# Four PSUM banks for the score products, and a new order of the first and last row blocks, in a two-layer graph kernel

## The chip, the cores and the metric

One core of one Trainium2 chip. The metric is the device time of one execution in microseconds; the median of three runs before the change is 658.79 us (658.75 to 659.19).

## The reference

`x` is 4096 x 128, `adj` is 4096 x 4096 with zeros and ones, `N` is 4096.

```
deg  = clip(adj.sum(1), 1);  dis = deg ** -0.5
diffusion = (dis[:, None] * adj * dis[None, :]) @ x - x
sim  = x @ x.T / (norms[:, None] * norms[None, :])
attn = softmax(beta * sim * adj, axis=1)
L0   = diffusion + sigmoid(alpha) * (attn @ x - x)
x    = layernorm(x + L0)
L1   = relu(adj @ (x @ weights))
out  = layernorm(x + L1)
```

## The kernel before, in words

Rows are handled in 32 **row blocks** `r` of 128 rows. Everything that belongs to an even block has `q = 0`, to an odd one `q = 1` (buffers of two). One row block of the attention goes through these steps; the name is that of the helper in the code, with its line.

- `land_piece` (SyncE, L242) brings a quarter of the block's adjacency rows into `land`. `cast` (ScalarE, L482) turns each quarter into bytes in `adj_bytes` and counts `cast_done`.
- `sign_block` (GpSimd, L321) makes the stationary operand. `cosines(r, q, h)` (TensorE, L1005) computes 512 columns of the scores of block `r` with three matmuls into one PSUM bank, for `h` from 0 to 7.
- `mask(r, q, h)` (VectorE, L708) multiplies that bank by the adjacency bytes into `scores` and counts `scores_done`. It waits for the cosines (`s_done`) and for the cast of its quarter, number `r*4 + h//2 + 1`. After eight of them `row_max` (L717, L719) gives the maximum.
- `exps` (ScalarE, L523) takes the exponential, a quarter at a time in the order 2, 3, 0, 1 (0, 2, 3, 1 in the first and last block).
- Half of the exponentials, `b` from 0 to 3, is transposed by TensorE: `turn_e` (L1016) into `ps_e[0]` or `ps_e[1]`, then split into a high and a low fp16 part by `e_high` (ScalarE, L530) and `e_low` (VectorE, L723). The other half is split first, by `ex_high` (GpSimd, L351) and `ex_low` (VectorE, L729, both tensor inputs in SBUF), and transposed by a DMA, `turn_ex` (SyncE, L254), into `eTx`.
- `attend(r, q, k)` (TensorE, L1038 and L1041) multiplies piece `order[k]` of the block by `x_parts`. `attn_add` (VectorE) adds the sum to `u`.
- `pack` (GpSimd, L331 to L343) and `turn_adj` (SyncE, L248) keep a packed, transposed adjacency matrix for the later phases.

From block 2 on these steps stand in a loop of two row blocks per turn, on every engine; in `row` TensorE issues, for each `h`, a `turn_e` (even `h`), one `cosines` of a block ahead and one `attend` of a block behind. The first blocks and the last two are written out by hand. Work that exists once stands among the first ones: `x_split`, `x_high` (GpSimd, L355 to L364) and `x_low(1)` (VectorE, L760, both tensor inputs in SBUF) make `x_parts`; `first_attend(2)` waits for `x_low(1)`. `minus_x` (GpSimd, L370) writes the start value of `u` in four pieces, and VectorE waits for all four before it enters its loop:

```
            row(1, 1, second=True)
            dve.wait_ge(u_init, C)
            with dve.Fori(2, R - 15, 2) as r:
```

After the attention come the diffusion sums (`sums` and `whole_row` on TensorE), the first normalisation, and the second layer (`z_rows`, `z_w`). `first_sums(i)`, the first of these, needs `y_low(i)` (VectorE, L819), which needs `y_high` (ScalarE) and `y_rows` (GpSimd, L443, both inputs in SBUF). They are issued among the last two row blocks, beside `late_attend` (block 30) and `last_attend` (block 31).

PSUM has eight banks: `ps_s[0..1]`, `ps_e[0..3]`, `ps_acc`, `ps_at`. In the first block scores go to `ps_s` and to `ps_e[0..3]`; from block 1 on to `ps_s[h % 2]` alone, so that `cosines` number `n` waits for `mask` number `n - 2`. `ps_e[2]` and `ps_at` are then unused until the sums.

## Time and profile before

| | us |
|---|---|
| median of 3 runs | 658.79 |
| the profiled execution, its own time | 658.59 |
| its span, first to last instruction | 656.7 |
| TensorE busy | 638.0 (97%) |
| VectorE busy | 517.8 (79%) |
| ScalarE busy | 412.2 (63%) |
| GpSimd busy | 236.8 (36%) |
| granted TensorE clock | 0.998 |

All times below are microseconds from the start of the span. The attention fills the first 427 us, of which the hand-written start is about 55 and the hand-written end about 25. Masks, `e_low` and `exps` in the rows below are told apart by their order in the code. A matmul's end is modelled; a step from one start to the next is the better measure of what TensorE takes.

### The profile page before, as it was taken

How to read it: one execution, taken by the hardware profiler on the slowest of the kernel's cores; microseconds unless marked ns; L12 is line 12 of the kernel's file. 1: busy time of each engine (PE TensorE's matmuls, PEld its weight loads, DVE VectorE, ACT ScalarE, POOL GpSimd, SP SyncE). 2: the span in 40 equal slices, each digit the busy share in tenths (PEclk: the TensorE clock that was granted, in tenths of full speed). 3: DMA queues.
4: the chain of work that ended last, by engine and by line, in shares of the span. 5: the costliest groups of instructions: out<-in, count | busy, mean ns of one | idle time of the engine just before them, and what ended most of it. 6: DMA issues, size and time to landing. Idle time of an engine off the chain costs nothing.

```text
span 656.7 us, 16155 instructions
## 1 busy us (share of the span) xinstructions
PE 638.0 (97%) x5087; PEld 463.5 (71%) x5087; DVE 517.8 (79%) x1565; ACT 412.2 (63%) x768; POOL 236.8 (36%) x249
## 2 busy tenths in 40 slices
PE   7788999999999999999999999999999999999996
PEld 6456777777777777777777777888888864444465
DVE  4987999999999999999999998878777773334443
ACT  6998999999999999999999998612111110000000
POOL 5998553553554554544544546400000000000000
PEclk9999999999999999999999999999999999999999
DMA  7878999999999999999999996300000000000000
GB/s 282 303 161 215 278 272 239 279 256 253 280 267 239 285 263 233 285 263 242 292 258 240 307 237 97 77 1 1 0 0 0 0 0 1 16 17 16 16 33 33
DMA packets 165019, 107.36 MB, mean 163 GB/s; under 512 B 144384, under 2 KB 148608, under 8 KB 164992
## 3 DMA queue, kind: packets, MB, share of 16 engines
q1 hardware_dynamic: 164992, 107.04, 61.6%
q8 instruction: 12, 0.20, 0.1%
q14 instruction: 15, 0.12, 0.1%
HBM read 69.27 MB, written 2.10 MB: 109 GB/s over the span
## 4 chain that ended last, share of the span: by engine, by line
PE 86%; DVE 4%; DMA 4%; ACT 2%; issue 2%; POOL 1%; DVEq 0%; SPq 0%; POOLq 0%; ACTq 0%
PE ps_s L1005 22%; PE ps_s L1198 17%; PE ps_e L1170 15%; PE ps_e L1016 8%; PE ps_e L1038 8%; PE ps_acc L1038 7%; PE ps_e L1041 4%; PE ps_acc L1041 4%; DMA eTx<-e_parts 2%; DVE scores L708 1%; DMA x_keep<-in_x 1%; PE ps_e L1054 1%; DVE e_parts L729 1%; PE ps_acc L1182 1%; PE ps_s L1054 1%
## 5 line engine op out<-in xcount | busy, mean ns | idle before, releaser
L1005 PE MATMUL ps_s<-xn_parts,xn_signed 128*128 128x512 f16 x756 | 203.3, 379 | 4.2 <-DVE cmax L708 4.2
L708 DVE CUSTOM_DVE_ANT_1 scores<-ps_s,adj_bytes 128x512 f32<-128x512 f32 x252 | 171.6, 683 | 24.4 <-PE ps_s L1005 15.2
L523 ACT ACTIVATE scores<-scores,col 128x1024 f32<-128x1024 f32 x128 | 157.4, 1232 | 2.1 <-DVE col L719 1.9
L482 ACT ACTIVATE adj_bytes<-land 128x1024 uint8<-128x1024 f32 x128 | 133.5, 1047 | 0.6 <-POOL packed L343 0.6
L351 POOL TENSOR_SCALAR e_parts<-scores 128x1024 f16<-128x1024 f32 x64 | 68.5, 1071 | 157.7 <-ACT scores L523 154.2
L1170 PE MATMUL ps_e<-y_parts,stage 128*128 128x256 f16 x896 | 98.0, 273 | 0.0
L1005 PEld LDWEIGHTS ps_s<-xn_parts,xn_signed 128*128 128x128 f16 x756 | 68.4, 98 | 40.2 <-DVE cmax L708 4.3
L1170 PEld LDWEIGHTS ps_e<-y_parts,stage 128*128 128x128 fp8e4 x896 | 87.7, 98 | 10.1
L530 ACT ACTIVATE eT_parts<-ps_e 128x512 f16<-128x512 f32 x128 | 75.8, 595 | 28.7 <-PE ps_e L1016 27.9
L723 DVE SCALAR_TENSOR_TENSOR eT_parts<-ps_e,eT_parts 128x512 f16<-128x512 f32 x128 | 87.4, 683 | 1.9 <-ACT eT_parts L530 1.9
L729 DVE SCALAR_TENSOR_TENSOR e_parts<-scores,e_parts 128x1024 f16<-128x1024 f32 x64 | 88.4, 1382 | 0.4 <-POOL e_parts L351 0.4
L1016 PE MATMUL ps_e<-ident,scores 128*128 128x128 f32 x512 | 77.0, 274 | 1.6 <-ACT scores L523 1.6
L619 ACT ACTIVATE scores<-ps_s 128x512 f32<-128x512 f32 (+1 forms) x9 | 4.9, 550 | 108.6 <-PE ps_s L1198 108.6
L596 ACT ACTIVATE std<-mv,col 128x1 f32<-128x1 f32 x32 | 9.4, 295 | 84.2 <-DVE mv L898 84.2
L1016 PEld LDWEIGHTS ps_e<-ident,scores 128*128 128x128 f32 x512 | 53.9, 140 | 4.4 <-ACT scores L523 1.6
L1198 PE MATMUL ps_s<-stage,x_parts 128*128 128x512 fp8e4 (+1 forms) x320 | 56.9, 336 | 0.0
L1198 PE MATMUL ps_s<-land,x_parts 128*128 128x512 fp8e4 x256 | 56.4, 379 | 0.0
L805 DVE TENSOR_SCALAR stage<-packT 128x256 uint32<-128x256 uint32 (+1 forms) x192 | 42.6, 287 | 14.7 <-PE ps_e L1170 11.8
L1038 PE MATMUL ps_acc<-x_parts,eT_parts 128*128 128x256 f16 x256 | 49.0, 273 | 1.6 <-DVE eT_parts L723 1.6
L340 POOL TENSOR_TENSOR packed<-packed,adj_bytes 128x256 uint32<-128x256 uint32 x48 | 49.1, 1023 | 2.7
L1038 PE MATMUL ps_e<-x_parts,eT_parts 128*128 128x256 f16 x256 | 49.0, 273 | 0.6 <-DVE eT_parts L723 0.6
L1038 PE MATMUL ps_acc<-x_parts,eTx 128*128 128x256 f16 x256 | 48.9, 273 | 0.6 <-DMA eTx<-e_parts 0.6
(128 smaller groups left out, 967.1 us busy)
## 6 DMA issues: line engine op xcount, KB each, us to landing
land<-in_adj SPq DMA_DIRECT2D x128, 512.0 KB, 5.4
x_keep<-in_x SPq DMA_DIRECT2D x4, 512.0 KB, 5.6
out<-u SPq DMA_DIRECT2D x7, 256.0 KB, 2.1
eTx<-e_parts SPq DMA_TRANSPOSE x64, 4.3
packT<-packed SPq DMA_TRANSPOSE x16, 6.5
out<-u SPq DMA_DIRECT2D x2, 128.0 KB, 1.7
scores<-in_L_gnn_weights SPq DMA_DIRECT2D x1, 64.0 KB, 2.0
col<-in_L_gnn_beta SPq DMA_DIRECT2D x1, 0.5 KB, 7.1
```

The costliest lines, as they stand in the source:

```text
L351: nc.gpsimd.tensor_scalar(e_parts[:, n, 0, :], scores[:, q, (n + 2) * CH:(n + 3) * CH], E_SCALE, 1.0, ALU.mult, ALU.mult).wait_op(sign_don ...
L482: nc.scalar.activation(adj_bytes[:, q, i * CH:(i + 1) * CH], land[:, q, i, :], ACT.Copy, scale=float(BYTE_TOP[q] >> i), accum_out=deg[:, i ...
L523: nc.scalar.activation(piece, piece, ACT.Exp, bias=neg_max[q], scale=abs_beta, accum_out=csum[:, q, i:i + 1]).then_inc(exp_done, 1)
L530: nc.scalar.activation(eT_parts[:, b, 0, :], ps_e[:, b % 2, :], ACT.Copy, scale=E_SCALE).then_inc(e_hi, 1)
L708: nc.vector.tensor_tensor_reduce(scores[:, q, o:o + BANK].rearrange("p (k q) -> p k q", k=K), score_bank(h, r == 0 if start else False).re ...
L723: nc.vector.scalar_tensor_tensor(eT_parts[:, b, 1, :], ps_e[:, b % 2, :], E_SCALE, eT_parts[:, b, 0, :], ALU.mult, ALU.subtract).then_inc( ...
L729: nc.vector.scalar_tensor_tensor(e_parts[:, n, 1, :], scores[:, q, (n + 2) * CH:(n + 3) * CH], E_SCALE, e_parts[:, n, 0, :], ALU.mult, ALU ...
L1005: ins = nc.tensor.matmul(score_bank(h, start), xn_signed[:, q, part, :], xn_parts[:, other, o:o + BANK], start=(part == 0 and other == 0), ...
L1016: ins = nc.tensor.transpose(ps_e[:, b % 2, n * P:(n + 1) * P], scores[:, q, t * P:(t + 1) * P], ident[:, :])
L1038: nc.tensor.matmul(attn_ps[q][:, 0:2 * D], hi, x_parts[:, t, :], start=(k == 0 and n == 0), stop=(k == H - 1 and n == TH - 1), skip_group_ ...
L1170: ins = nc.tensor.matmul(ps_e[:, n, 0:2 * D], stage8[n][:, b, :, k], y_tiles[t], start=(t == 0), stop=(t == R - 1))
L1198: ins = nc.tensor.matmul(ps_s[:, q, 0:rows * P], x_parts[:, t, part * D:(part + 1) * D], quads8[q if rows == G else 1][:, b, k, n:n + rows ...
```

## The change

Scores of row block 1 and later go to four banks in turn, `ps_s[0]`, `ps_s[1]`, `ps_e[2]`, `ps_at`, and `cosines` number `n` waits for `mask` number `n - 4`. The other edits change the order in which the hand-written parts issue the same instructions: SyncE, ScalarE, VectorE and TensorE at the start, VectorE, TensorE and GpSimd at the end. Nothing is added or left out. The pieces of the diff are, after the table and the bank function, SyncE, GpSimd's end, ScalarE (two places), VectorE's start, VectorE's end, and TensorE.

```diff
-    LATE_ATTEND = (0, 4, 5, 1, 6, 7, 2, 3)
+    LATE_ATTEND = (0, 4, 5, 1, 2, 6, 7, 3)
...
         def score_bank(h, start):
-            return ps_e[:, h - 2 if h < 4 else h - 4, :] if start and h % 4 >= 2 else ps_s[:, h % 2, :]
+            if h % 4 < 2:
+                return ps_s[:, h % 2, :]
+            if start:
+                return ps_e[:, h - 2 if h < 4 else h - 4, :]
+            return ps_e[:, 2, :] if h % 4 == 2 else ps_at[:, :]
...
             turn_ex(1, 1, 0)
+            def row_4(i):
+                sp.wait_ge(cast_done, 2 * C + i + 1)
+                land_piece(1, 0, i)
+            row_4(0)
+            row_4(1)
             turn_adj(0, 0)
+            turn_ex(1, 1, 1)
+            row_4(2)
+            row_4(3)
+            turn_ex(2, 0, 0)
-            for k in range(G):
+            for k in range(1, G):
                 turn(1, k)
...
+            y_rows(2)
             ex_high(R - 1, 1, 0, place=1)
             ex_high(R - 1, 1, 1, place=1)
-            y_rows(2)
             y_rows(3)
...
             norm_root(0)
+            norm_root(1)
             squares(2)
-            norm_root(1)
...
             cast(2, 0, 0)
+            exps(1, 1, 2)
             cast(2, 0, 1)
-            exps(1, 1, 2)
             exps(1, 1, 3)
...
             row_max(0, 0)
-            mask(1, 1, 0, start=True)
-            mask(1, 1, 1, start=True)
-            x_low(1)
+            for h in range(4):
+                mask(1, 1, h, start=True)
             e_low(0, 0)
-            mask(1, 1, 2, start=True)
-            mask(1, 1, 3, start=True)
+            mask(1, 1, 4, start=True)
             e_low(0, 1)
             ex_low(0, 0, 0)
-            mask(1, 1, 4, start=True)
             mask(1, 1, 5, start=True)
             ex_low(0, 0, 1)
-            e_low(0, 2)
             mask(1, 1, 6, start=True)
             mask(1, 1, 7, start=True)
             row_max(1, 1)
+            e_low(0, 2)
+            mask(2, 0, 0)
             e_low(0, 3)
-            mask(2, 0, 0)
+            x_low(1)
             mask(2, 0, 1)
...
             e_low(R - 1, 0)
-            ex_low(R - 1, 1, 0)
             e_low(R - 1, 1)
             y_low(1)
+            ex_low(R - 1, 1, 0)
             ex_low(R - 1, 1, 1)
...
                 elif not start:
-                    pe.wait_ge(scores_done, r * H + (h - 1))
+                    pe.wait_ge(scores_done, r * H + (h - 3))
...
             cosines(1, 1, 1)
+            cosines(1, 1, 2)
+            cosines(1, 1, 3)
             turn_e(0, 0, 0, True, FIRST_EXP)
             turn_e(0, 0, 1, True, FIRST_EXP)
-            cosines(1, 1, 2)
-            cosines(1, 1, 3)
             cosines(1, 1, 4)
+            cosines(1, 1, 5)
             first_attend(0)
-            cosines(1, 1, 5)
+            cosines(1, 1, 6)
             first_attend(1)
             turn_e(0, 0, 2, True, FIRST_EXP)
             turn_e(0, 0, 3, True, FIRST_EXP)
-            cosines(1, 1, 6)
             cosines(1, 1, 7)
+            cosines(2, 0, 0)
+            cosines(2, 0, 1)
             first_attend(2)
-            cosines(2, 0, 0)
             first_attend(3)
-            cosines(2, 0, 1)
+            cosines(2, 0, 2)
             first_attend(4)
-            cosines(2, 0, 2)
             cosines(2, 0, 3)
             row(1, 1, second=True)
```

VectorE at the start, from the second mask of row block 1: before. L708 is a mask (the row after it reads its maximum), L760 is `x_low(1)`, L723 is `e_low`, L729 is `ex_low`.

```order
L708 ISA scores,cmax<-ps_s,adj_bytes 128x512
L708 ISA cmax 128x1
L760 SCALAR_TENSOR_TENSOR x_parts<-x_keep,col,x_parts 128x8x128
L723 SCALAR_TENSOR_TENSOR eT_parts<-ps_e,eT_parts 128x512
L708 ISA scores,cmax<-ps_s,adj_bytes 128x512
L708 ISA cmax 128x1
L708 ISA scores,cmax<-ps_s,adj_bytes 128x512
L708 ISA cmax 128x1
L723 SCALAR_TENSOR_TENSOR eT_parts<-ps_e,eT_parts 128x512
L729 SCALAR_TENSOR_TENSOR e_parts<-scores,e_parts 128x1024
```

The same place now, from the third mask of row block 1 (a mask is now L723, `e_low` L738, `ex_low` L744, `x_low` L775, `row_max` L732 and L734):

```order
L723 ISA scores,cmax<-ps_e,adj_bytes 128x512
L723 ISA cmax 128x1
L723 ISA scores,cmax<-ps_at,adj_bytes 128x512
L723 ISA cmax 128x1
L738 SCALAR_TENSOR_TENSOR eT_parts<-ps_e,eT_parts 128x512
L723 ISA scores,cmax<-ps_s,adj_bytes 128x512
L723 ISA cmax 128x1
L738 SCALAR_TENSOR_TENSOR eT_parts<-ps_e,eT_parts 128x512
L744 SCALAR_TENSOR_TENSOR e_parts<-scores,e_parts 128x1024
```

Four masks come first, `mask(1, 1, 4)` stands between the first two `e_low`, and `x_low(1)` is gone from here. It stands further down, from the last mask of row block 1 on:

```order
L723 ISA scores,cmax<-ps_at,adj_bytes 128x512
L723 ISA cmax 128x1
L732 TENSOR_REDUCE col<-cmax 128x1
L734 TENSOR_SCALAR col<-col 128x1
L738 SCALAR_TENSOR_TENSOR eT_parts<-ps_e,eT_parts 128x512
L723 ISA scores,cmax<-ps_s,adj_bytes 128x512
L723 ISA cmax 128x1
L738 SCALAR_TENSOR_TENSOR eT_parts<-ps_e,eT_parts 128x512
L775 SCALAR_TENSOR_TENSOR x_parts<-x_keep,col,x_parts 128x8x128
```

`e_low(0, 2)`, `e_low(0, 3)` and `x_low(1)` now all come behind the `row_max` of block 1. At the end, VectorE from `e_low(31, 0)`: before,

```order
L723 SCALAR_TENSOR_TENSOR eT_parts<-ps_e,eT_parts 128x512
L729 SCALAR_TENSOR_TENSOR e_parts<-scores,e_parts 128x1024
L723 SCALAR_TENSOR_TENSOR eT_parts<-ps_e,eT_parts 128x512
L819 TENSOR_TENSOR y_parts<-x_keep,y_parts 128x8x128
L729 SCALAR_TENSOR_TENSOR e_parts<-scores,e_parts 128x1024
```

and now:

```order
L738 SCALAR_TENSOR_TENSOR eT_parts<-ps_e,eT_parts 128x512 x2
L832 TENSOR_TENSOR y_parts<-x_keep,y_parts 128x8x128
L744 SCALAR_TENSOR_TENSOR e_parts<-scores,e_parts 128x1024 x2
L738 SCALAR_TENSOR_TENSOR eT_parts<-ps_e,eT_parts 128x512 x2
L751 SCALAR_TENSOR_TENSOR u<-ps_acc,col,u 128x128
```

`y_low(1)` (L819, now L832) has moved ahead of the first `ex_low` of the last block.

## Rows read from the trace of the kernel before

**Rows 1.** The page, part 1: busy time, share of the span and instructions of TensorE.
```profile
PE   638.0 (97%) x5087; PEld 463.5 (71%) x5087; DVE 517.8 (79%) x1565; ACT 412.2 (63%) x768; POOL 236.8 (36%) x249
```

**Rows 2.** Busy time by stretch, 200 to 300 us.
```profile
200.00:300.00 100.00, 99.99 (x850) 73.16 (x848) 93.85 (x243) 93.27 (x164) 49.88 (x53) 1.00 1.01 262
```

**Rows 3.** Timeline of TensorE, 21 to 70 us: start, duration, what, idle time before.
```profile
24.26 1.46 PE L1005 MATMUL ps_s<-xn_parts,xn_signed 128*128 128x512 f16 x6 [1.34 <-DVE cmax L708]
26.59 1.09 PE L1016 MATMUL ps_e<-ident,scores 128*128 128x128 f32 x8 [0.88 <-ACT scores L523]
...
30.05 0.82 PE L1005 MATMUL ps_s<-xn_parts,xn_signed 128*128 128x512 f16 x3 [1.07 <-DVE cmax L708]
...
31.37 0.81 PE L1005 MATMUL ps_s<-xn_parts,xn_signed 128*128 128x512 f16 x3
...
41.38 0.60 PE L1016 MATMUL ps_e<-ident,scores 128*128 128x128 f32 x4
...
60.09 0.82 PE L1005 MATMUL ps_s<-xn_parts,xn_signed 128*128 128x512 f16 x3 [1.24 <-DVE cmax L708]
...
69.42 0.65 PE L1016 MATMUL ps_e<-ident,scores 128*128 128x128 f32 x4 [0.18 <-ACT scores L523]
```

**Rows 4.** Waits of TensorE, 41 to 70 us: total, times, longest.
```profile
PE ps_s L1005 <- DVE cmax L708: 1.8, 2, 1.2
PE ps_e L1016 <- ACT scores L523: 0.8, 2, 0.6
```

**Rows 5.** Timeline of ScalarE, 29 to 66 us.
```profile
29.85 1.05 ACT L482 ACTIVATE adj_bytes<-land 128x1024 uint8<-128x1024 f32 x1
...
37.49 1.24 ACT L523 ACTIVATE scores<-scores,col 128x1024 f32<-128x1024 f32 x1 [0.93 <-DVE col L719]
...
65.03 1.24 ACT L523 ACTIVATE scores<-scores,col 128x1024 f32<-128x1024 f32 x1 [0.99 <-DVE col L719]
```

**Rows 6.** Timeline of VectorE, 26 to 65 us.
```profile
26.90 1.88 DVE L760 SCALAR_TENSOR_TENSOR x_parts<-x_keep,col,x_parts 128x1024 f16<-128x1024 f32 x1
...
30.53 0.68 DVE L723 SCALAR_TENSOR_TENSOR eT_parts<-ps_e,eT_parts 128x512 f16<-128x512 f32 x1
31.13 1.58 DVE L729 SCALAR_TENSOR_TENSOR e_parts<-scores,e_parts 128x1024 f16<-128x1024 f32 x1
...
42.98 1.22 DVE L729 SCALAR_TENSOR_TENSOR e_parts<-scores,e_parts 128x1024 f16<-128x1024 f32 x1
...
59.34 0.69 DVE L708 CUSTOM_DVE_ANT_1 scores<-ps_s,adj_bytes 128x512 f32<-128x512 f32 x1 [2.68 <-ACT adj_bytes L482]
...
64.78 0.21 DVE L719 TENSOR_SCALAR col<-col 128x1 f32<-128x1 f32 x1
```

**Rows 7.** Timeline of GpSimd, 25 to 59 us.
```profile
25.57 2.14 POOL L364 TENSOR_TENSOR x_parts<-u,x_parts 128x1024 f16<-128x1024 f32 x1
27.93 2.89 POOL L351 TENSOR_SCALAR e_parts<-scores 128x1024 f16<-128x1024 f32 x2 [0.23 <-ACT scores L523]
...
31.71 1.60 POOL L334 TENSOR_TENSOR packed<-packed,adj_bytes 128x256 uint32<-128x256 uint32 x1
33.38 0.73 POOL L343 TENSOR_TENSOR packed<-packed,adj_bytes 128x256 uint32<-128x256 uint32 x1
...
38.02 2.14 POOL L364 TENSOR_TENSOR x_parts<-u,x_parts 128x1024 f16<-128x1024 f32 x1
...
57.65 1.13 POOL L370 TENSOR_SCALAR u<-x_keep,col 128x1024 f32<-128x1024 f32 x1
```

**Rows 8.** The DMA transposes `turn_ex`, 30 to 80 us, from issue to landing.
```profile
DMA to landing us min/median/max: 4.3/4.6/5.7
```

**Rows 9.** Timelines of VectorE and TensorE, last row block.
```profile
419.79 1.21 DVE L729 SCALAR_TENSOR_TENSOR e_parts<-scores,e_parts 128x1024 f16<-128x1024 f32 x1
...
417.69 0.28 PE L1038 MATMUL ps_e<-x_parts,eT_parts 128*128 128x256 f16 x1 [0.63 <-DVE eT_parts L723]
...
425.43 0.28 PE L1038 MATMUL ps_e<-x_parts,eTx 128*128 128x256 f16 x1
```

## The prediction

> **What bounds the kernel now.** I read the page's busy times first: TensorE is busy for 638.0 of 656.7 us [rows 1]. Then the busy time by stretch: from 200 to 300 us TensorE is busy for 99.99 of 100 us, with VectorE and ScalarE at 93% [rows 2]. So in the loop the matmuls themselves set the time, and neither a wait for a score bank nor an order of the others costs anything there. What a new order can change is TensorE's idle time outside the loop. The timeline of TensorE is where to see it: in the start it stands still four times for a score bank, before the matmuls at 24.26, 30.05 and 60.09 and once more between 41 and 55 [rows 3, 4], for the exponentials at 26.59 and 69.42 and once between [rows 3, 4], and for other things a few times more. In the loop there is nothing to be had; what is left is in the last two row blocks.
>
> The last thing to read is what releases the last of these waits, at 69.42. It is the `turn_e` of row block 3, which needs three exponentials that began at 65.03, which needed the row maximum that VectorE wrote at 64.78 to 64.99 [rows 3, 5, 6]. VectorE came to that maximum in 5.6 us of nearly unbroken work after it had stood still for 2.68 us until 59.34 [rows 6]. The trace names a cast there, but the cast that this mask needs was long done. The wait that stands in the code just there is the one for the four `minus_x`, and the fourth ran on GpSimd from 57.65 to 58.78 [rows 7]. GpSimd had been at work without a gap worth naming from 27.93 on. So **GpSimd's chain from 27.93 to 58.78 decides when the loop gets going**, and TensorE's waits before 60 us are slack against it.
>
> **The start, step by step.** *Banks.* With four banks, cosines of block 1 wait for masks of block 0 that end before 24.9. Four of them fit before the transposes at 26.59, which wait for exponentials that do not move (same ScalarE order so far). The wait of 1.34, that of 1.07 and the later ones for a bank (1.8 in two) go: 4.2 us of idle time that the four banks take away [rows 3, 4]. What takes their place is below.
>
> *VectorE.* A mask or an `e_low` takes 0.60 from start to start (30.53 to 31.13 [rows 6]). Four masks, begun at 25.2 as before, end at 27.6; `e_low(0, 0)` waits for ScalarE until 28.3 and ends at 28.95. Next stands `mask(1, 1, 4)`, which needs the cast that ScalarE runs from 29.85 to 30.9 [rows 5]; with the read of its sum it is 31.03. **Here VectorE stands for 2.1 us**, with `e_low(0, 1)` and `ex_low(0, 0, 0)` queued behind it. From 31.03: mask and `e_low` 1.2, `ex_low` 1.2 (as at 42.98 [rows 6]), mask, `ex_low`, two masks, maximum: about 36.65 to 37.1 against 37.45 before, a gain of 0.4 in the maximum. But `e_low(0, 2)`, `e_low(0, 3)`, a mask and `x_low(1)` now come after it, so `x_low(1)` is ready to start at 38.9.
>
> *The shared port.* At 26.90 `x_low` took 1.88, and it ran beside GpSimd's L364, which ended at 27.71; 1.07 are left after that. The packing step at 31.71 took 1.60 where the next one took 0.73 [rows 6, 7], and the `ex_low` that VectorE ran from 31.13 to 32.71 ended inside it. I read this as one at a time, first come first: a VectorE operation with two SBUF inputs waits for the GpSimd operation that has begun, and then holds the next one up for about 1.1. Now `x_low(1)` comes at 38.9 into the second such L364, which will run from about 38.3 to 40.4 (before: 38.02 to 40.15 [rows 7]). It then runs from 40.4 to 41.6 and holds GpSimd for 1.1. Before, it cost GpSimd 0.2, because the second `ex_high` of the pair at 27.93 (2.89 for both) had to wait for its exponentials anyway. So GpSimd is 0.9 later at least. Followed on through five more `ex_low`, which hit it in new phases (the one of block 2 comes later with VectorE and holds up the last `minus_x`), it is 1.6 later: the fourth `minus_x` ends at 60.4.
> The Trainium skill (SBUF — State Buffer, Who interferes with whom) says that a VectorE instruction with two SBUF inputs contends with a GpSimd instruction that reads SBUF. It also says that masks, with one SBUF input, do not. By that rule, the trace agrees.
>
> *ScalarE.* `exps(1, 1, 2)` now stands ahead of `cast(2, 0, 1)`. Before, ScalarE idled 0.93 until 37.49 [rows 5]; now it idles two us and runs the 1.04 of the cast later. All exponentials of block 1 but the first are 0.8 later. This hides behind TensorE, which is later still.
>
> *TensorE.* `first_attend(2)` waits for `x_low(1)`, so it starts at 41.8. A cosines and an attend take 0.66 each (30.05 to 31.37 for both [rows 3]). Three attends and two cosines follow, so the first `turn_e` of block 1 starts at 45.1 against 41.38 [rows 3]: 3.7 later. Between there and 69.42 TensorE had 2.6 us of shown idle time for banks and exponentials [rows 4], some 3.5 with the small gaps and the modelled ends. Taken away, its own work brings it to 69.6. So without GpSimd's delay it would be a tie at 69.4; with it the maximum of block 3, its exponentials and its `turn_e` come 1.6 later (chain as before, 59.34 to 69.42). I take 1.4, since some of VectorE's small waits on the matmuls go with the banks. Bounds: -0.2 (no delay, and the 0.18 at 69.42 goes) and +2.6 (one more 1.1 collision).
>
> *SyncE.* Two loads of block 4 are issued ahead of `turn_adj(0, 0)` and `turn_ex(1, 1, 1)`. That transpose is issued at about 52 and needed at 58.2; a transpose lands 4.3 to 5.7 after its issue [rows 8], so 57.7 at worst: nothing. If that cover is gone it costs what it is late, up to 1.
>
> *First microseconds.* `norm_root(1)` comes 0.6 earlier; the third `unit_rows` still waits for the third norm: 0.
>
> **The loop.** TensorE full before and after [rows 2]: 0, with 0.3 either way.
>
> **The end.** `late_attend` in the new order gains at most 0.25, as its last piece waits for `e_low(30, 3)`. `e_low(31, 1)` and `y_low(1)` come earlier, so the wait of 0.63 at 417.69 [rows 9] and one like it behind it go. But both `ex_low` of block 31 now end at about 419.5 and 420.7, behind `y_low(1)` and its collision with the last `y_rows`, where the first ended four us earlier and the second at 421.0 [rows 9]. The two DMA transposes thus follow each other on SyncE's queue, which the first holds for 1.8 to 2.9. The last piece needs the second: 421.4 plus 4.3 is 425.7 or later, against 425.43 [rows 8, 9]. I take +0.2; bounds -0.8 and +1.3. What was won in front becomes a wait for the last transpose.
>
> **The sum.** 0 + 1.4 + 0 + 0.2 = +1.6 on the profiled execution's 658.59, or 660.2. The median of the runs stands 0.2 above that execution, so I say 660.4.
>
> **Rivals.** A measurement of this kernel can tell about 0.2%, or 1.3 us, from no change.
> *A, slower (this forecast), 40%:* GpSimd's chain takes the `x_low` collision and the loop starts later; 660.2 to 662.5. It is decided by whether the fourth `minus_x` ends after 59.9.
> *B, no change, 34%:* the delay of GpSimd is 0.5 or less, because the collisions fall into phases that cost nothing or the end gives back what the start loses. For it speaks that TensorE arrives at 69.6 on its own work; 657.5 to 660.1, most likely 659.
> *C, faster, 26%:* the 2.68 us of VectorE before 59.34 are not GpSimd's but an effect of the tight banks, and the chain moves up with TensorE. Then the bank wait of 1.24 comes back, 0.18 with it, and at the end up to 0.8 [rows 3]: 2.2 in all at most, 656.4 to 657.4. Against it stands the order of the code and that 58.78 fits.
> *That the edit does nothing* is excluded in one respect only: the banks do change the waits, as the code of both sides says; in the loop it does nothing, which is part of all three.
>
> **Range.** From just under C's 656.4, so 656.3, to A's upper bound, 658.8 + 2.6 + 1.3 less a little, 662.4. B and A hold most of it; A alone would be 660.2 to 662.5.
>
> **What would show it.** Right: TensorE has no wait for a bank after 24 us; VectorE idles about 2 us before a mask at 31.0; `x_low` starts near 39 and takes over 2.5; the first `turn_e` of block 1 is at about 45; the mask after `minus_x` is at about 61, not 59.34; the `turn_e` of block 3 at about 71, not 69.42; the last transposed piece at 425.7 plus the shift of the start. Wrong: `x_low` at 1.2 to 1.9 without a wait, or VectorE past `minus_x` before 59.3, or a row maximum of block 3 before 64.8. The sign then turns with the chain.

## The result, and the profile after

The changed kernel takes 665.64 us (median of 4 runs, 664.74 to 666.50) against 658.88 for the kernel before: a ratio of 1.0097 with a 95% interval of 1.0082 to 1.0112, so 6.8 us slower. The forecast was 660.4 with a range to 662.4: the right side, far too small. The profiled execution took 664.74, its span is 662.8.

Page, part 1, and the stretch from 200 to 300 us, of the kernel after.
```profile
PE 640.6 (97%) x5087; PEld 465.5 (70%) x5087; DVE 519.2 (78%) x1565; ACT 412.7 (62%) x768; POOL 237.3 (36%) x249
...
200.00:300.00 100.00, 100.00 (x852) 73.28 (x851) 93.77 (x241) 93.16 (x164) 49.61 (x53) 1.00 1.03 259
```
The loop is as full as before [rows 2]. TensorE is busy for 2.6 us more [rows 1] with the same instructions, which is the first sign of a lower clock.

The timelines give four points that cut the time into five parts. The shift of each is the loss in its part:

| | before | after | loss in the part |
|---|---|---|---|
| first mask (VectorE) | 18.54 | 19.96 | 1.42 |
| row maximum of block 3 | 64.58 | 70.36 | 4.36 |
| row maximum of block 31 | 406.91 | 412.30 | -0.39 |
| the last transposed piece (TensorE) | 425.43 | 431.52 | 0.70 |
| end (own time of the execution) | 658.59 | 664.74 | 0.06 |

So 5.8 of the 6.15 are lost before the loop is under way (the row maximum of block 3 falls into its first turn). Timeline of TensorE, after.
```profile
16.60 1.97 PE L1002 MATMUL ps_e<-ident,scores 128*128 128x128 f32 x8
18.36 2.10 PE L1018 MATMUL ps_s<-xn_parts,xn_signed 128*128 128x512 f16 x6
...
43.85 0.37 PE L1051 MATMUL ps_acc<-x_parts,eT_parts 128*128 128x256 f16 x1 [6.26 <-DVE x_parts L775]
...
48.62 0.60 PE L1029 MATMUL ps_e<-ident,scores 128*128 128x128 f32 x4
...
75.20 0.65 PE L1029 MATMUL ps_e<-ident,scores 128*128 128x128 f32 x4 [1.53 <-ACT scores L538]
```
Not one wait for a score bank is left [rows 3, 4]. In their place TensorE stands once for 6.26 us, for `x_low(1)`, and before that once for 2.01, for an `e_low`. The first `turn_e` of block 1 is at 48.62 (41.38 before), the one of block 3 at 75.20 (69.42 before).

Busy time by stretch, after. Behind the length of the stretch stands TensorE's busy time with its count; the granted clock is third from the end.
```profile
17.00:19.00 2.00, 2.00 (x10) 1.60 (x9) 0.97 (x4) 0.99 (x2) 1.45 (x2) 0.50 1.02 412
...
38.00:40.00 2.00, 0.00 (x0) 0.00 (x0) 1.93 (x8) 0.06 (x1) 1.85 (x2) 1.00 1.22 185
...
42.00:46.00 4.00, 2.15 (x14) 1.72 (x15) 3.45 (x10) 4.00 (x9) 3.68 (x5) 0.50 0.51 107
```
Twice the granted clock is 0.50, that is 1.2 GHz. Both times TensorE had stood before: for 0.84 until 13.85 and for 1.09 until 16.14, with short work between, and then all of the time from 37.6 to 43.85. The kernel before has the same wait of 1.09, until 16.34, and its clock stayed at 1.00 there, so the short waits alone do not explain the first fall. The eight transposes at 16.60 took 1.97 and the six matmuls at 18.36 took 2.10, against 1.09 and 1.46 for the same kinds at full clock [rows 3]: 1.5 more together, where the first mask is 1.42 later. From 43.85 to 48.62 stand three attends and two cosines, 4.77 us in place of the 3.3 that they take at full clock.

Timelines of VectorE and GpSimd, after. L723 is a mask, L744 `ex_low`, L775 `x_low(1)`; L366 is `ex_high`, L355 packing, L385 `minus_x`.
```profile
32.58 0.69 DVE L723 CUSTOM_DVE_ANT_1 scores<-ps_s,adj_bytes 128x512 f32<-128x512 f32 x1 [2.19 <-ACT adj_bytes L497]
...
36.12 2.12 DVE L744 SCALAR_TENSOR_TENSOR e_parts<-scores,e_parts 128x1024 f16<-128x1024 f32 x1
...
41.63 2.08 DVE L775 SCALAR_TENSOR_TENSOR x_parts<-x_keep,col,x_parts 128x1024 f16<-128x1024 f32 x1
...
65.12 0.69 DVE L723 CUSTOM_DVE_ANT_1 scores<-ps_s,adj_bytes 128x512 f32<-128x512 f32 x1 [2.79 <-ACT adj_bytes L497]
```
```profile
41.59 1.05 POOL L366 TENSOR_SCALAR e_parts<-scores 128x1024 f16<-128x1024 f32 x1
42.72 3.19 POOL L355 TENSOR_TENSOR packed<-packed,adj_bytes 128x256 uint32<-128x256 uint32 x3
...
53.16 2.10 POOL L385 TENSOR_SCALAR u<-x_keep,col 128x1024 f32<-128x1024 f32 x1
58.04 1.05 POOL L366 TENSOR_SCALAR e_parts<-scores 128x1024 f16<-128x1024 f32 x1 [2.78 <-ACT scores L538]
59.18 1.12 POOL L385 TENSOR_SCALAR u<-x_keep,col 128x1024 f32<-128x1024 f32 x1
62.30 1.05 POOL L366 TENSOR_SCALAR e_parts<-scores 128x1024 f16<-128x1024 f32 x1 [2.00 <-DMA eTx<-e_parts]
63.43 1.12 POOL L385 TENSOR_SCALAR u<-x_keep,col 128x1024 f32<-128x1024 f32 x1
```
The chain of the forecast is there: the fourth `minus_x` ends at 64.55, the mask behind it starts at 65.12 after 2.79 of idle time (58.78 and 59.34 before [rows 6, 7]). Its four ends tell where it fell behind: the first is at 49.90 (49.83 before), the second 2.0 later than before (two collisions with `ex_low`, in the packing step at 49.88 and the `minus_x` at 53.16), the third 4.7 (a wait of 2.78 for exponentials), the fourth 5.8 (a wait of 2.00 for a transposed piece, of which the `ex_high` behind it gave back 0.84: it took 1.05, and 1.89 before). Before, GpSimd had neither wait.

The queue that this piece came through, SyncE's, after: L246 is a load, L252 `turn_adj`, L258 `turn_ex`.
```profile
38.85 14.12 SPq L258 DMA_TRANSPOSE eTx<-e_parts  x2
53.03 1.46 SPq L246 DMA_DIRECT2D land<-in_adj  x2
54.59 1.19 SPq L252 DMA_TRANSPOSE packT<-packed  x1
55.88 3.58 SPq L258 DMA_TRANSPOSE eTx<-e_parts  x1
```
`turn_ex(1, 1, 1)` is issued at 55.88, behind both loads, and a transpose took up to 6.2 here to land (median 4.4): at 62.1, and `ex_high` at 62.30 had waited for it since 60.30.

The last row blocks, after: VectorE, SyncE and TensorE.
```profile
421.69 4.05 DVE L744 SCALAR_TENSOR_TENSOR e_parts<-scores,e_parts 128x1024 f16<-128x1024 f32 x2
...
424.68 4.94 SPq L258 DMA_TRANSPOSE eTx<-e_parts  x2
...
431.52 0.28 PE L1051 MATMUL ps_e<-x_parts,eTx 128*128 128x256 f16 x1 [0.98 <-DMA eTx<-e_parts]
```
Both `ex_low` of block 31 follow each other, so do their transposes, and TensorE waits for the second one, where it did not before [rows 9].

### The profile page after: what moved, and what is told of

Its sections match the earlier page's. It is cut to its first block, busy times and chain, and to the rows that moved or that the text cites. A ratio compares the mean times of both kernels' runs of the same rounds, so it can differ in the third digit from the quotient of the medians.

```text
span 662.8 us, 16155 instructions
## 1 busy us (share of the span) xinstructions
PE 640.6 (97%) x5087; PEld 465.5 (70%) x5087; DVE 519.2 (78%) x1565; ACT 412.7 (62%) x768; POOL 237.3 (36%) x249
## 4 chain that ended last, share of the span: by engine, by line
PE 91%; DVE 4%; ACT 3%; DMA 1%; issue 1%; SPq 0%; DVEq 0%; ACTq 0%
PE ps_s L1211 17%; PE ps_e L1183 15%; PE ps_s L1018 12%; PE ps_e L1029 8%; PE ps_e L1051 8%; PE ps_acc L1051 8%; PE ps_e L1018 6%; PE ps_at L1018 6%; PE ps_e L1054 4%; PE ps_acc L1054 4%; ACT scores L538 1%; DMA eTx<-e_parts 1%; PE ps_e L1067 1%; DVE e_parts L744 1%; DVE scores L723 1%
## 5 line engine op out<-in xcount | busy, mean ns | idle before, releaser
L366 POOL TENSOR_SCALAR e_parts<-scores 128x1024 f16<-128x1024 f32 x64 | 67.0, 1046 | 161.9 <-ACT scores L538 156.3
L1018 PE MATMUL ps_s<-xn_parts,xn_signed 128*128 128x512 f16 x384 | 103.6, 381 | 0.1
L723 DVE CUSTOM_DVE_ANT_1 scores<-ps_s,adj_bytes 128x512 f32<-128x512 f32 x128 | 87.4, 684 | 14.8 <-issue 5.7
L744 DVE SCALAR_TENSOR_TENSOR e_parts<-scores,e_parts 128x1024 f16<-128x1024 f32 x64 | 90.4, 1413 | 0.0
L738 DVE SCALAR_TENSOR_TENSOR eT_parts<-ps_e,eT_parts 128x512 f16<-128x512 f32 x128 | 87.3, 684 | 1.6 <-ACT eT_parts L545 1.6
L723 DVE CUSTOM_DVE_ANT_1 scores<-ps_e,adj_bytes 128x512 f32<-128x512 f32 x66 | 45.1, 686 | 13.2 <-PE ps_e L1018 13.2
L1018 PE MATMUL ps_e<-xn_parts,xn_signed 128*128 128x512 f16 x198 | 53.5, 381 | 0.0
L1051 PE MATMUL ps_e<-x_parts,eTx 128*128 128x256 f16 x256 | 49.0, 273 | 2.1 <-DMA eTx<-e_parts 2.1
L355 POOL TENSOR_TENSOR packed<-packed,adj_bytes 128x256 uint32<-128x256 uint32 x48 | 49.4, 1029 | 2.7
```

The source lines that it names most:

```text
L366: nc.gpsimd.tensor_scalar(e_parts[:, n, 0, :], scores[:, q, (n + 2) * CH:(n + 3) * CH], E_SCALE, 1.0, ALU.mult, ALU.mult).wait_op(sign_don ...
L723: nc.vector.tensor_tensor_reduce(scores[:, q, o:o + BANK].rearrange("p (k q) -> p k q", k=K), score_bank(h, r == 0 if start else False).re ...
L738: nc.vector.scalar_tensor_tensor(eT_parts[:, b, 1, :], ps_e[:, b % 2, :], E_SCALE, eT_parts[:, b, 0, :], ALU.mult, ALU.subtract).then_inc( ...
L744: nc.vector.scalar_tensor_tensor(e_parts[:, n, 1, :], scores[:, q, (n + 2) * CH:(n + 3) * CH], E_SCALE, e_parts[:, n, 0, :], ALU.mult, ALU ...
L1018: ins = nc.tensor.matmul(score_bank(h, start), xn_signed[:, q, part, :], xn_parts[:, other, o:o + BANK], start=(part == 0 and other == 0), ...
L1051: nc.tensor.matmul(attn_ps[q][:, 0:2 * D], hi, x_parts[:, t, :], start=(k == 0 and n == 0), stop=(k == H - 1 and n == TH - 1), skip_group_ ...
```

## The experiments

Theory S (start): the time goes by GpSimd's chain up to the fourth `minus_x`, which the late `x_low(1)` pushes back. Its rivals: TensorE's own path behind `x_low(1)`, its lower clock, SyncE's order, the four banks, the tail. The kernel before ran beside each set, at medians of 659.3 to 659.6, and at 658.88 beside the changed kernel. Its single executions lie up to 3.6 us apart, so ratios are given with their intervals; where two medians of different sets are subtracted, up to 0.7 us can be the sets' own difference.

### The parts taken back one at a time

**`norm_root` as before.**
```
             norm_root(0)
-            norm_root(1)
             squares(2)
+            norm_root(1)
```


> The changed kernel with one thing undone: norm_root(1) stands behind squares(2) on ScalarE again. Clock theory: the clock stays at 2.4 GHz from 13 to 20 us, the first mask starts at 18.5 again instead of 19.96, and the 1.4 us come off the end: about 664.2. Rival (the 1.4 us are hidden behind x_low and the transposes of the start): the first mask moves, the time stays within 0.3 of 665.6.

Measured: 664.28, ratio 1.0066 (1.0050 to 1.0083), 1.4 less than with it. The interval touches that of the changed kernel, so its share is not settled. Its profiled execution, the longest of the four (667.21), does not show the gain: the clock was full until 42 us, but the first mask came at 19.37 and not at 18.5, and from there to the row maximum of block 3 it took 52.20 (50.40 in the changed kernel). It does name the releaser itself. Timeline of VectorE.
```profile
66.32 0.69 DVE L723 CUSTOM_DVE_ANT_1 scores<-ps_s,adj_bytes 128x512 f32<-128x512 f32 x1 [3.33 <-POOL u L385]
```
The first mask of the loop waits for `minus_x` by name here, where the rows of before named a cast [rows 6].

**SyncE as before** (loads of block 4 behind `turn_adj(0, 0)` and `turn_ex(1, 1, 1)`).
```
-            row_4(0)
-            row_4(1)
             turn_adj(0, 0)
-            turn_ex(1, 1, 1)
-            row_4(2)
-            row_4(3)
-            turn_ex(2, 0, 0)
...
-            for k in range(1, G):
+            for k in range(G):
                 turn(1, k)
```


> The changed kernel with SyncE's order undone: the loads of row block 4 come behind turn_ex(1, 1, 1) again. Transpose theory: GpSimd's wait of 2.00 us for the transposed piece before 62.30 goes, minus_x ends about 2 us earlier, and the end with it: about 663.7. Rival (VectorE or TensorE is as late by itself): minus_x earlier, time within 0.4 of 665.6.

Measured: 661.16, ratio 1.0039 (1.0015 to 1.0064). Seven of ten runs lay at 660.2 to 662.1, three at 665.9 to 666.7 with a mean clock of 0.985 to 0.987. The profile is of one of the three (666.64). GpSimd's timeline in it, then two stretches.
```profile
59.73 1.05 POOL L356 TENSOR_SCALAR e_parts<-scores 128x1024 f16<-128x1024 f32 x1 [2.79 <-ACT scores L528]
60.86 1.12 POOL L375 TENSOR_SCALAR u<-x_keep,col 128x1024 f32<-128x1024 f32 x1
62.07 1.05 POOL L356 TENSOR_SCALAR e_parts<-scores 128x1024 f16<-128x1024 f32 x1
63.20 1.97 POOL L375 TENSOR_SCALAR u<-x_keep,col 128x1024 f32<-128x1024 f32 x1
```
```profile
16.00:24.00 8.00, 7.11 (x25) 4.09 (x26) 5.30 (x16) 6.20 (x12) 7.04 (x8) 0.58 0.98 369
42.00:50.00 8.00, 5.59 (x29) 3.71 (x30) 4.71 (x13) 6.40 (x12) 7.42 (x8) 0.58 0.38 94
```
The wait for the transposed piece is gone, the one for the exponentials stays. The gain is not in this execution: the fourth `minus_x` ends at 65.17, and from the first mask (20.80) to the row maximum of block 3 it takes 50.19, against 50.40 in the changed kernel. Its clock was lower and for longer. None of the seven shorter executions was profiled, so where they gained is not shown.

**`x_low(1)` into VectorE's gap.**
```
             e_low(0, 0)
+            x_low(1)
             mask(1, 1, 4, start=True)
...
             e_low(0, 3)
-            x_low(1)
             mask(2, 0, 1)
```


> The changed kernel with x_low(1) put into VectorE's idle time ahead of mask(1, 1, 4). Theory that the late x_low costs: first_attend(2) starts before 42 instead of 43.85, the clock does not fall a second time at 41 us, and 2 to 3 us come off: 662.6 to 663.6. Rival (the transpose on SyncE decides alone): time within 0.4 of 665.6.

Measured: 660.52, ratio 1.0016 (1.0000 to 1.0033): **5.1 of the 6.8 us** by moving one instruction, 2 more than expected. VectorE, then GpSimd.
```profile
30.21 1.28 DVE L775 SCALAR_TENSOR_TENSOR x_parts<-x_keep,col,x_parts 128x1024 f16<-128x1024 f32 x1
...
60.56 0.69 DVE L723 CUSTOM_DVE_ANT_1 scores<-ps_s,adj_bytes 128x512 f32<-128x512 f32 x1 [2.69 <-ACT adj_bytes L497]
```
```profile
57.03 1.75 POOL L366 TENSOR_SCALAR e_parts<-scores 128x1024 f16<-128x1024 f32 x1 [0.35 <-DMA eTx<-e_parts]
```
`x_low` runs in the gap that the new order itself leaves before the fifth mask, in 1.28; GpSimd was idle for 0.65 of that, and its next `ex_high` took 1.44 in place of 1.05. TensorE never stands for it, no second fall of the clock follows, and GpSimd's wait for the transposed piece is 0.35 in spite of SyncE's new order.

### The parts put alone on the kernel before

**`norm_root` alone** (the two lines above, the other way round).

> The kernel before with one thing added: norm_root(1) ahead of squares(2). Clock theory: the clock falls to half at 16 to 20 us, the first mask starts at 19.9 instead of 18.5, and the time is 1.0 to 1.4 us longer: about 660.1. Rival (harmless reorder, the drop has another cause): clock full, time 658.8.

Measured: 659.75, ratio 1.0001 (0.9991 to 1.0012). Nothing. In the profiled execution the clock fell between 16 and 20 us and the first mask came at 19.76; in others the mean clock was 1.000. The same fall showed in an execution with the old order (first mask at 19.61, below) and was missing in one with the new (18.41). Five of the seven profiled executions with the new order have it, and one of the ten with the old; the times do not show it, so whether the new order makes it more frequent stays open.

**Four banks alone.**
```
-            return ps_e[:, h - 2 if h < 4 else h - 4, :] if start and h % 4 >= 2 else ps_s[:, h % 2, :]
+            if h % 4 < 2:
+                return ps_s[:, h % 2, :]
+            if start:
+                return ps_e[:, h - 2 if h < 4 else h - 4, :]
+            return ps_e[:, 2, :] if h % 4 == 2 else ps_at[:, :]
...
-                    pe.wait_ge(scores_done, r * H + (h - 1))
+                    pe.wait_ge(scores_done, r * H + (h - 3))
```

> The kernel before with the four banks alone, no order changed. Theory that the start hangs on GpSimd's four minus_x (end at 58.8): the waits for a bank before 30.05, 42.51 and 60.09 go, minus_x and the turn_e of row block 3 stay at 58.8 and 69.4, and the time is within 0.4 of the kernel before. Rival (the bank waits are on the path): 1 to 3 us faster.

Measured: 660.26, ratio 1.0013 (1.0002 to 1.0024). TensorE's timeline.
```profile
69.33 0.65 PE L1020 MATMUL ps_e<-ident,scores 128*128 128x128 f32 x4 [1.53 <-ACT scores L527]
```
The waits for a bank are gone and the `turn_e` of block 3 stays where it was (69.42 [rows 3]): 1.24 and 0.18 have become one wait of 1.53 for the exponentials. In the start the banks were slack, as forecast. The time is 0.8 above the kernel before, where 0.4 was allowed for, and that is in the tail: 19.68 from the row maximum of block 31 to the last transposed piece, against 18.52. There the second `ex_low` of block 31 took 2.91, behind a `y_rows` of GpSimd, in place of 1.21 [rows 9], and TensorE waited 0.91 for the piece.

**`x_low(1)` late alone.**
```
             mask(1, 1, 1, start=True)
-            x_low(1)
             e_low(0, 0)
...
             e_low(0, 3)
+            x_low(1)
             mask(2, 0, 0)
```


> The kernel before with one thing moved: x_low(1) behind e_low(0, 3) instead of behind the second mask of row block 1. Theory that the late x_low costs by itself: TensorE stands before first_attend(2) for 3 to 5 us, the clock falls after it, and the time is 1 to 4 us longer. Rival (only harmful together with SyncE's order): within 0.4 of the kernel before.

Measured: 662.93, ratio 1.0042 (1.0026 to 1.0059). TensorE's timeline, and two stretches.
```profile
38.79 0.37 PE L1038 MATMUL ps_acc<-x_parts,eT_parts 128*128 128x256 f16 x1 [4.32 <-DVE x_parts L760]
```
```profile
36.00:40.00 4.00, 1.21 (x8) 0.98 (x9) 2.57 (x6) 4.00 (x7) 3.85 (x3) 0.73 0.98 233
40.00:44.00 4.00, 4.00 (x17) 2.05 (x16) 0.70 (x2) 4.00 (x8) 3.67 (x5) 0.50 0.25 57
```
Behind a stand of 4.32 the clock was 0.50 here too. GpSimd then waited 2.79 for exponentials, the fourth `minus_x` ended at 61.74, and from the first mask to the row maximum of block 3 it took 49.18, against 46.04 before. So the late `x_low(1)` alone costs 3.5 us.

**SyncE alone** (the lines above, the other way round).

> The kernel before with SyncE's new order alone. Transpose theory: turn_ex(1, 1, 1) goes behind two loads and turn_adj, lands later than GpSimd wants it, ex_high(2, 0, 1) waits, and the time is 0.5 to 2 us longer. Rival (in the kernel before the loads are ready too late to delay anything, or early enough to hide): within 0.3.

Measured: 659.45, ratio 0.9999 (0.9987 to 1.0010), no wait of GpSimd for a transposed piece. Taking this order back had brought 4.5. So by the medians it costs only where `x_low` is late as well: the second transpose of block 1 is then issued two loads late and lands after GpSimd wants its buffer. 2.0 of that are visible as the wait at 62.30; where the rest of the 4.5 comes from was not found. The seven shorter executions without the order also had mean clocks of 0.993 to 0.997, the changed kernel 0.991 to 0.994.

**Three parts back** (`x_low` in the gap, SyncE and `norm_root` as before; banks, ScalarE and tail as changed).

> The changed kernel with three things undone or mended: x_low(1) in VectorE's idle time, SyncE's order and norm_root as before. If these three carry the loss, it is at 658.6 to 659.3, level with the kernel before; if the order of exps and casts and the end cost too, it stays 0.5 to 1.5 us above.

Measured: 659.99, ratio 1.0010 (0.9998 to 1.0022). What is left of the change is a tie within the interval, 0.6 above the kernel before in the same set, with a tail of 19.23.

**The tail alone.**
```
-    LATE_ATTEND = (0, 4, 5, 1, 6, 7, 2, 3)
+    LATE_ATTEND = (0, 4, 5, 1, 2, 6, 7, 3)
...
+            y_rows(2)
             ex_high(R - 1, 1, 0, place=1)
             ex_high(R - 1, 1, 1, place=1)
-            y_rows(2)
...
-            ex_low(R - 1, 1, 0)
             e_low(R - 1, 1)
             y_low(1)
+            ex_low(R - 1, 1, 0)
             ex_low(R - 1, 1, 1)
```

> The kernel before with the changed order of the last two row blocks alone (VectorE, GpSimd, TensorE). Prediction: the last transposed piece 0.3 later, +0.2 on the time (bounds -0.8 and +1.3), within what can be measured. Rival: the tail alone costs 1 or more, by the wait of the last attend for the second transpose.

Measured: 660.26, ratio 1.0017 (1.0005 to 1.0028). From the row maximum of block 31 to the last transposed piece it takes 19.25 in this profile, 19.22 in the changed kernel and 18.52 before: +0.7. The banks alone had lengthened it by 1.16, so the two do not add up.

### The clock against the delay

```
+            for _ in range(40):
+                nc.tensor.matmul(ps_acc[:, 2 * D:2 * D + P], ident[:, :], ident[:, :], start=True, stop=True)
             first_attend(2)
```


> The changed kernel with 40 small matmuls of 128 columns (result in a part of the bank that nobody reads) ahead of the third attend of row block 0, inside TensorE's stand of 6.26 us. Theory clock: part of the price of the late x_low is that TensorE comes out of its stand at 1.2 GHz; with the filler the granted clock stays 1.0 from 37 to 48 us, the three attends and two cosines behind x_low take 3.3 us instead of 4.8, the exponentials of block 1 and the GpSimd ex_high behind them come about 1 earlier, and the time falls by 1 to 1.5, to 664.2 to 664.7. Rival: the clock of that stretch costs nothing, because the chain goes over SyncE's transpose and GpSimd: full clock, the fourth minus_x still at 64 to 65, time as before the edit (665.6).

Measured: 668.65, ratio 1.0143 (1.0124 to 1.0163). The filler was too long. TensorE's timeline.
```profile
36.29 9.09 PE L1124 MATMUL ps_acc<-ident 128*128 128x128 f32 x80
45.22 0.27 PE L1051 MATMUL ps_acc<-x_parts,eT_parts 128*128 128x256 f16 x1
```
40 matmuls in f32 are 80 records of 0.11 us; they ran 2.7 past the end of `x_low` (42.56). The clock was held at 1.00, but this run does not tell the theories apart. Of the 4.0 by which its profiled execution exceeds the changed kernel's, 0.1 lie before the row maximum of block 3 (the first mask 1.13 earlier, the stretch behind it 1.22 longer), 0.6 in the loop and 3.4 in the tail and behind, where TensorE waited 2.73 for the last transposed piece (0.98 in the changed kernel); why is not known, as the filler does not reach there. With 18 in place of the 40:

> The changed kernel with 18 small matmuls in the stand in place of the 40, which took 9.09 us (each stands in the trace as two records, 0.23 us for both) and themselves ran 2.7 us past x_low. 18 take 4.1 us and end at about 41.7 in the profiled execution's time, before x_low does. Theory clock: granted clock 1.0 from 40 to 48 us, first turn_e of block 1 about 4.9 behind the start of the third attend no more but 3.3; the exponentials behind come 1.4 earlier, the time 1 to 1.5 shorter: 664.2 to 664.7. Rival: the chain over GpSimd does not follow, time as before the edit (665.6).

Measured: 664.30, ratio 1.0067 (1.0045 to 1.0090), 1.3 less than the changed kernel. TensorE, then GpSimd.
```profile
43.92 0.27 PE L1051 MATMUL ps_acc<-x_parts,eT_parts 128*128 128x256 f16 x1 [1.25 <-DVE x_parts L775]
...
47.19 0.60 PE L1029 MATMUL ps_e<-ident,scores 128*128 128x128 f32 x4
```
```profile
62.65 1.05 POOL L366 TENSOR_SCALAR e_parts<-scores 128x1024 f16<-128x1024 f32 x1 [3.54 <-DMA eTx<-e_parts]
```
The stretch behind `x_low` is 3.27 instead of 4.77, as the clock theory says. The median says about 1.3 (the ratios 2.0), but the intervals overlap, and in the profiled execution the gain was swallowed: GpSimd waited 3.54 for the transposed piece, and from the first mask to the row maximum of block 3 it took 50.34 (50.40 in the changed kernel). So the second fall of the clock costs between nothing and 2. The other falls count as well: with the filler, the two executions with a mean clock of 0.999 took 662.71 and 663.10, the two with 0.992 and 0.993 took 667.09 and 665.49. The greater part of the loss is the delay itself: in the two executions at 0.999 the kernel is still 3.4 and 3.8 us behind the kernel before (659.34 in that set).

### The wait for `minus_x` itself

`attn_add` of row block `r` needs only the piece of `u` with its own rows, eight row blocks to a piece. VectorE can enter its loop with two pieces:
```
-            dve.wait_ge(u_init, C)
+            dve.wait_ge(u_init, 2)
             with dve.Fori(2, R - 15, 2) as r:
                 row(r, 0)
+                dve.wait_ge(u_init, C)
                 row(r + 1, 1)
```
In the kernel before:

> The kernel before with the same finer wait. Theory (the chain of GpSimd sets the loop's entry): the 2.68 us of VectorE before 59.34 go, the first mask of the loop at 56.8 to 57.5, the turn_e of row block 3 at 68 to 69 and the time 0.5 to 1.5 shorter, as TensorE's own work then decides. Rival C of the prediction (the 2.68 us are an effect of the banks): no change, 658.6 to 659.4.

Measured: **656.63**, ratio 0.9957 (0.9944 to 0.9970), **2.7 us faster than the kernel before**, and more than the 1.5 expected at most. VectorE, GpSimd and TensorE.
```profile
57.74 0.69 DVE L708 CUSTOM_DVE_ANT_1 scores<-ps_s,adj_bytes 128x512 f32<-128x512 f32 x1 [0.15 <-DVE e_parts L729]
```
```profile
58.58 1.12 POOL L370 TENSOR_SCALAR u<-x_keep,col 128x1024 f32<-128x1024 f32 x1
```
```profile
68.38 0.60 PE L1017 MATMUL ps_e<-ident,scores 128*128 128x128 f32 x4
```
VectorE starts the mask before the fourth `minus_x` has begun, and TensorE reaches the `turn_e` of block 3 without a wait. From the first mask to the row maximum of block 3 it takes 43.40 us in place of 46.04: 2.64, the gain of the median. This is the chain that the forecast named for the kernel before, now shown by taking its last link away.

In the changed kernel:

> The changed kernel in which VectorE waits for two minus_x ahead of the loop and for the other two inside its first round, behind row block 2 (u rows 8 and up are not used before). Theory: the loop's entry hangs on the fourth minus_x; the first mask of the loop comes at about 62.5, when its cast and cosines are there, row_max(3) by up to 2.5 earlier and the time is 1.5 to 2.5 shorter: about 663.5. Rival: the four minus_x only end at the same time as the rest, the masks behind wait for cosines or signs of GpSimd instead, and the time stays at 665.6.

Measured: 663.36, ratio 1.0058 (1.0039 to 1.0077), 2.3 less than without it; 47.90 for the same stretch in place of 50.40. TensorE's timeline.
```profile
42.28 0.27 PE L1052 MATMUL ps_acc<-x_parts,eT_parts 128*128 128x256 f16 x1 [4.58 <-DVE x_parts L775]
47.22 0.60 PE L1030 MATMUL ps_e<-ident,scores 128*128 128x128 f32 x4
...
71.68 0.61 PE L1030 MATMUL ps_e<-ident,scores 128*128 128x128 f32 x4
```
The finer wait takes about the same from both kernels, so it leaves the loss where it was: 663.36 against 656.63, 6.7 us, and in the stretch 47.90 against 43.40, 4.50 (4.36 with the whole wait). **With `minus_x` out of the way the late `x_low` costs as much by TensorE's own path.** From the first `turn_e` of block 1 at 47.22 to that of block 3 at 71.68 TensorE waits for nothing: 24.46 of its own work. In the changed kernel that work, from 48.62 on, would end at 73.1; the `minus_x` chain put another 2.1 on top, to 75.20.

With the four banks on the kernel before:

> The kernel before with the finer wait for minus_x and the four banks. Theory (rival C's idea, once minus_x is off the chain): TensorE's own work now decides, the bank waits were 3 to 4 us of it, so the banks now bring something: the turn_e of row block 3 by 0.3 to 1 earlier than the 68.1 of the finer wait alone, time 655.6 to 656.4. Rival: the exponentials decide in turn, as at the wait of 1.53 that the four banks alone had; no difference to the finer wait alone, 656.6.

Measured: 657.57, ratio 0.9970 (0.9955 to 0.9984). No gain over the finer wait alone, with the banks' lengthened tail (19.65); the stretch from the first mask to the row maximum of block 3 is 43.54, against 43.40. Even with `minus_x` off the chain, the exponentials take over from the banks: the last wait of TensorE before the `turn_e` of block 3 is in both kernels one for the exponentials of block 2 (0.66 with the banks, 0.57 without), and from there it is 12.27 in both.

With three parts of the change back:

> The changed kernel with x_low(1) in VectorE's gap, SyncE's order and norm_root as before, and the finer wait. Theory: it keeps the banks and the cast and tail orders; the finer wait takes from 659.99 the same 2.7 as from the kernel before: 657 to 657.6, slower than the finer wait on the kernel before by the tail's 0.9. Rival: the reordered masks leave less slack elsewhere and only 1 is gained, 659.

Measured: 657.95, ratio 0.9977 (0.9966 to 0.9987), 2.0 less than without the finer wait and 1.3 behind the kernel before with it. The best version stays the kernel before with the finer wait.

## Why the prediction was wrong, point by point

**What bounds it: right for the kernel before, half right for the changed one.** GpSimd's chain to the fourth `minus_x` decided the loop's entry in both kernels; the finer wait gave 2.7 and 2.3 us by that alone. The banks bought nothing, alone or with it. But the loss does not hang on that chain: without it the changed kernel is still 6.7 us behind. **"Without GpSimd's delay it would be a tie at 69.4" is the step that failed on TensorE's side.** The forecast had its first `turn_e` of block 1 at 45.1 and 24.5 of work behind it; the 24.5 were right (24.46), the start was 48.62. Of these 3.5, 2.0 are the later `first_attend(2)` (43.85 for 41.8) and 1.5 the clock behind the stand (4.77 for 3.3).

**Masks and the gap: half right.** VectorE stood 2.19 before the fifth mask of block 1 (forecast 2.1). But the two `ex_low` behind it took 1.79 and 2.12, where I took 1.2 each: they met GpSimd's packing and x scaling. The row maximum of block 1 came 1.0 later than before, counted from the first mask, not 0.4 earlier.

**The step that failed first: "`x_low(1)` is ready to start at 38.9", run from 40.4 to 41.6.** It ran from 41.63 to 43.71: 2.1 later at its end, of which 1.4 is the later first mask and the rest the slow `ex_low`. It met an `ex_high` (41.59 to 42.64) and then needed 1.07 alone; the packing behind waited until it was done. First come, first served held, though the `ex_high` was only 0.04 ahead, but with another partner than I had named. The Trainium skill (SBUF — State Buffer, Who interferes with whom) says that the port pair that VectorE shares with GpSimd is an exclusive lock, and that issue order, not the kind of operation, decides who blocks. By that rule, the trace agrees, 1.28 in the gap against 2.08 here included.

**The step that failed most on GpSimd's side: "1.6 later" for the fourth `minus_x`.** It was 5.8. I had followed the collisions, which came to 2.0 by the second `minus_x`, but had taken GpSimd to be busy throughout. With TensorE 7.2 late at the first `turn_e` of block 1 (forecast 3.7), GpSimd ran out of work: it waited 2.78 for exponentials and 2.00 for a transposed piece. A chain that is full before a change need not be full after it.

**"SyncE: nothing": wrong in company, right alone.** I reckoned the transpose at 52 with 5.7 to land against a need at 58.2. It was issued at 55.88, as its `ex_low` was late too and the loads stood ahead of it, and needed at 60.3. That 2.00 is the wait that the forecast had put at nothing; what the order is worth beyond it stays open.

**TensorE's clock: left out.** The forecast had `first_attend(2)` at 41.8, which means a stand of some four us, but priced the work behind it at full clock. Behind the stand of 6.26 the granted clock was 0.50. The Trainium skill (TensorE: Matmul & The Clock Gate, HAM oscillation — how this bites in real kernels) says that a wait for a DMA's data can leave TensorE to start its next burst at the lower clock. By that rule the third attend starts at 1.2 GHz, and the trace agrees.

**First microseconds: 0 forecast, 1.42 in the profiled execution**, by a fall of the clock that came in some executions, with the old order and with the new, and not in others; the first mask lay between 17.81 and 20.80 in the experiments. How much of this part belongs to the change and how much to the single execution stays open. **Loop: right** (-0.39; over all profiled executions this part lies between 341.9 and 343.6). **End: mechanism right, +0.7 for +0.2**: the last attend waited for the second of two transposes in a row. But the banks, which the forecast gave no part in the end, bring the same wait by themselves (+1.16).

The sum: 3.0 more than forecast in the start proper (4.36 for 1.4), 1.4 in the first microseconds, 0.5 in the tail, 0.3 less in the loop and behind: 4.6, from the forecast's 1.6 to the 6.15 measured.

## What to carry to other kernels

Before reordering, look at what the last wait before the loop is for, and whether it asks for more than the loop's first turns use: here a finer wait, two lines, was worth 2.7 us, and the whole reordering less than nothing. A chain that decides the loop's entry need not be what a change makes slower: its last link was worth 2.7 us in one kernel and 2.3 in the other, and the 6.7 between them stayed, as a second chain was just as late. An instruction that another engine waits for belongs in the gap that the new order opens, not behind work that only fills it. When the forecast makes one engine several us late, price everything behind it again: its clock after the stand, its own work up to the loop, and each queue that had been hidden by the engine being on time.

## What was not expected of the hardware

- TensorE's granted clock was 0.50 behind stands of 6.26 and of 4.32 us, in some executions already between 16 and 20 us, where it had only stood in short pieces, and in others for some us between 26 and 40. Executions of one kernel differ in it. It came back while TensorE was at work again.
- A 128-column matmul in f32 stands in the trace as two records of 0.11 us at full clock: 40 of them are 9.1 us.
- The same order of DMA issues cost nothing in one kernel (ratio 0.9999), and in another, with a late VectorE, the median was 4.5 us lower without it; 2.0 of that can be seen as a wait.
